# A three-layer macaron block on one core: attention's output sums leave by DMA on GpSimd's queue instead of through TensorE, and the next batches' LayerNorm and the queries' parts move to GpSimd

## What is computed

```python
x = x + 0.5 * ffn(layernorm(x))      # mixture of 8 experts, capacity 320, with a dense overflow path
x = x + attention(layernorm(x))
x = x + 0.5 * ffn(layernorm(x))
```

```python
xd = (x @ W_down).reshape(b, t, h, s)
keys = einsum('bthk,hik->bthi', xd, tokeys) * scale
queries = einsum('bthk,hik->bthi', xd, toqueries) * scale
values = einsum('bthk,hik->bthi', xd, tovalues)
attn = softmax(einsum('bqhs,bkhs->bhqk', queries, keys), axis=-1)
out = einsum('bhqk,bkhs->bqhs', attn, values).reshape(b, t, e)
return out @ W_unify + b_unify
```

## Time and profile before

| | |
|---|---|
| median of 3 runs | 2886.42 us |
| the profiled execution | 2896.95 us, its span 2895.2 us |
| attention, from the mask's first MEMSET to the last VectorE addition | 640.1 to 2259.1 us of the span |
| first exponential, last exponential | 707.1 and 2244.1 us |
| batches 1 to 6, first exponential to first exponential | 194.0 us each |
| batch 0 | 191.8 us |
| mean granted TensorE clock, whole program and inside batches | 0.964 and 1.00 |

### The profile page before, as it was taken

The page is one execution under the profiler, slowest core; times in us unless marked ns, Lnnn a source line. Parts: engine busy times, 40 slices in busy tenths (PEclk is TensorE's granted clock), DMA queues, the critical chain, the costliest instruction groups (busy, mean ns, idle before and its releaser), DMA issues. The chain is left out here.

```text
span 2895.2 us, 48611 instructions
## 1 busy us (share of the span) xinstructions
PE 2705.7 (93%) x17009; PEld 1644.3 (57%) x17009; DVE 2145.9 (74%) x3552; ACT 1821.3 (63%) x3409; POOL 599.8 (21%) x562
## 2 busy tenths in 40 slices
PE   5899999867999999999999999999999589999997
PEld 3799999863334334333343343433433368999886
DVE  6555456747899898998998988989895665554574
ACT  5344556632777776777777767777777444444564
POOL 3355114521100100101001001010000235521353
PEclk9899999986999999999999999999999789999998
DMA  5211113414123132131231321312310512111341
GB/s 172 66 44 44 58 45 106 133 60 75 30 50 75 33 61 54 39 62 36 50 75 33 60 55 39 62 37 50 60 28 5 173 30 80 44 44 45 102 133 63
DMA packets 164529, 181.69 MB, mean 63 GB/s; under 512 B 38472, under 2 KB 133904, under 8 KB 164368
## 3 DMA queue, kind: packets, MB, share of 16 engines
q1 hardware_dynamic: 156176, 169.03, 24.0%
q0 software_dynamic: 8192, 10.57, 1.2%
HBM read 97.51 MB, written 31.54 MB: 45 GB/s over the span
## 5 line engine op out<-in xcount | busy, mean ns | idle before, releaser
L1457 ACT ACTIVATE at_ex<-at_pd 128x512 f32<-128x512 f32 x2048 | 1084.7, 600 | 383.7 <-PE at_pd L1360 379.2
L1521 DVE TENSOR_REDUCE at_mxc<-at_pb 128x2 f32<-128x1024 f32 x1024 | 1219.0, 1219 | 120.8 <-PE at_pb L1349 113.8
L768 DVE TENSOR_TENSOR f_ml_hl<-f_ml_h,f_ml_hh 128x512 fp32r<-128x512 f32 (+1 forms) x384 | 287.8, 751 | 422.7 <-ACT f_ml_hh L844 421.5
L1360 PE MATMUL at_pd<-at_qa,at_ka 50*128 50x512 f32 x2048 | 583.6, 469 | 3.9 <-ACT at_ex L1457 3.2
L1360 PEld LDWEIGHTS at_pd<-at_qa,at_ka 50*128 50x128 f32 x2048 | 266.6, 185 | 538.4 <-issue 349.2
L1369 PE MATMUL at_po<-at_ex,at_va 128*32 128x512 f32 x4096 | 548.8, 608 | 0.2 <-ACT at_ex L1457 0.2
L841 ACT ACTIVATE f_ml_h<-f_ml_pL,b1T 128x512 f32<-128x512 f32 (+1 forms) x384 | 243.8, 635 | 457.9 <-PE f_ml_pL L895 446.3
L1349 PE MATMUL at_pb<-at_ka,at_qa 48*128 48x512 f32 x2048 | 433.1, 450 | 24.7 <-DVE at_mxc L1521 16.5
L910 PE MATMUL f_ml_pA<-f_wh,f_ml_hh 128*128 128x256 f32 (+1 forms) x1408 | 410.4, 291 | 3.7 <-DVE f_ml_hl L768 3.7
L912 PE MATMUL f_ml_pA<-f_wl,f_ml_hh 128*128 128x256 f32 (+1 forms) x1408 | 402.5, 286 | 0.0
L913 PE MATMUL f_ml_pA<-f_wh,f_ml_hl 128*128 128x256 f32 (+1 forms) x1408 | 402.5, 286 | 0.0
(11 more groups left out here) (128 smaller groups left out, 2636.6 us busy)
## 6 DMA issues: line engine op xcount, KB each, us to landing
f_wraw<-in_L_ffn_w SPq DMA_DIRECT2D x128, 256.0 KB, 2.8
at_qa<-at_parts SPq DMA_DIRECT2D x384, 64.0 KB, 2.4
at_ka<-at_parts SPq DMA_DIRECT2D x384, 64.0 KB, 2.4
f_ro_xr<-in_L_attn_x SPq DMA_DIRECT2D x16, 512.0 KB, 3.9
f_ml_xr<-in_L_attn_x SPq DMA_DIRECT2D x16, 512.0 KB, 4.2
x<-f_ml_yo SPq DMA_DIRECT2D x16, 512.0 KB, 4.0
at_xr<-x SPq DMA_DIRECT2D x16, 512.0 KB, 5.1
at_xres<-x SPq DMA_DIRECT2D x8, 1024.0 KB
```

Source lines behind the costliest of these rows:

```text
L768: eng.tensor_tensor(hl[h % RING][:, 0:w], h32[h % 2][:, 0:w], hh[h % RING][:, 0:w].bitcast(F32), ALU.subtract).then_inc(s_lo.sem, 1)
L1360: eng.matmul(pd[n % RING][:, :], ka[g][rows, p, kt * P:(kt + 1) * P], qa[g][rows, qh, p, :], start=True, stop=True).then_inc(s_full.sem, 1)
L1457: eng.activation(ex[t % 2][:, j, :], pd[n % RING][:, :], ACT.Exp).then_inc(s_free[n % RING].sem, 1)
L1521: eng.tensor_reduce(mxc[:, t // NT, kh, t % NT::NT], pb[kh][:, :].rearrange("p (e k) -> p e k", e=2), AX.X, ALU.max, negate=True).then_inc ...
```

## The change

- **The sums go by DMA.** `f` and `aT` leave the table. After `values_out` GpSimd issues, for each half unit, one DMA of `os_` to DRAM (`sums_out`), one that brings the totals back as 128 by 16 (`sums_in`, into `tot`), one that brings the values back already in the transposed place (`sums_in`, into `aT`). VectorE takes the reciprocal of `tot` (`reciprocals`, in step 4 or 12 of the half that follows), GpSimd stores it (`totals_out`) and reads it back spread over the 16 rows of each head (`totals_in`, into `den`). After two units' halves GpSimd multiplies `aT` by `den` (`divide`). The five DMAs and the multiplication stand in steps 0, 1, 5, 6 and 7 of the following half. Only the last half of the last batch goes the old way (`values_now`).
- **Output.** `u` of both halves is now in unit 0 of the next batch (steps 2, 3, 11, 12); of the last batch, half 0 is in steps 14 and 15 of unit 3.
- **LayerNorm a batch ahead.** Statistics of batch b + 2 are taken by VectorE in unit 0 (steps 13, 14) and unit 1 (steps 1, 2) of batch b, the variances in unit 2 (steps 2, 3); GpSimd normalises (`normalize`) in unit 2, steps 7 and 10.
- **Queries' parts.** ScalarE copies a `qk` bank to `xT` (freed by then), scaled; GpSimd makes both parts from there (`two_parts`).
- The bias is added to `xres` in unit 3 in two portions; `s_ld` and `s_mr` semaphores are merged; SyncE loads the rows of batch b + 3 in unit 3.

```diff
-        OUT = lambda f: [("aT", f, 0), ("aT", f, 1), ("u", f, 0), ("u", f, 1)]
+        PARTS = 2 * len(XD) + 2 * len(QK)
+        OUT = lambda f: [("u", f, 0), ("u", f, 1)]
...
-            table = {1: ("f", 1), 9: ("f", 0)}
-            if g == 0 and not prev:
-                del table[1]
+            table = {}
             if g == 0 and prev:
-                table.update(zip((2, 3, 5, 6), OUT(1)))
-            if g == 3:
-                table.update(zip((10, 11, 13, 14), OUT(0)))
+                table.update(zip((2, 3, 11, 12), OUT(0) + OUT(1)))
+            if g == 3 and last:
+                table.update(zip((14, 15), OUT(0)))
             if g == 0 and not last:
-                table.update(zip((7, 8, 10, 11, 13, 14), XT + XD))
+                table.update(zip((6, 7, 8, 9, 13, 14), XT + XD))
             if g == 1 and not last:
-                table.update(zip((2, 3, 5, 6, 7, 8), XD[-2:] + QK))
+                table.update(zip((1, 2, 5, 6, 7, 8), XD[-2:] + QK))
...
                 if j == 0:
-                    eng.wait_ge(s_free[n % RING].sem, s_free[n % RING].at(ring.freed(n)))
-                    eng.wait_ge(s_kp.sem, s_kp.at(2 * len(XD) * b + len(XD) * (c + 1)))
+                    eng.wait_ge(s_kp.sem, s_kp.at(PARTS * b + 2 * len(XD) + len(QK) * (c + 1)))
...
                 else:
                     f, h = a.at
+                    eng.wait_ge(s_dv.sem, s_dv.at(4 * a.b + 3 + f))
...
+            def reciprocals(b, g, qh):
+                eng.wait_ge(s_td.sem, s_td.at(16 * (half(b, g, qh) + 1)))
+                eng.reciprocal(tot[:, :], tot[:, :]).then_inc(s_rc.sem, 1)
...
             def values_out(b, g, t):
                 eng.wait_ge(s_pv.sem, s_pv.at(ST * unit(b, g) + t + 1))
+                if half(b, g, t // NT):
+                    eng.wait_ge(s_os.sem, s_os.at(16 * half(b, g, t // NT)))
                 eng.tensor_copy(os_[:, :], po[:, :]).then_inc(s_o.sem, 1)
...
-                    if g == 0 and not last and t < 8:
-                        f, q = t // 4, t % 4
-                        if q < 2:
-                            stats(b + 1, f, (FIRST, SECOND)[q])
-                        else:
-                            apply(self.ring, b + 1, f, side, (FIRST, SECOND)[q - 2])
+                    if t == NT + 4:
+                        reciprocals(b, g, 0)
+                    if t == 4 and (b or g):
+                        reciprocals(*before(b, g), 1)
+                    if (g, t) in STATS_AT and b + 2 < NBAT:
+                        stats(b + 2, STATS_AT[g, t])
+                    if (g, t) in VARIANCE_AT and b + 2 < NBAT:
+                        variance(b + 2, VARIANCE_AT[g, t])
...
+                eng.tensor_copy(parts[:, int(key), 0, c, at], src[:, c, at]).then_inc(s_kp.sem, 1)
+                eng.wait_ge(s_kp.sem, s_kp.at(n + 1))
+                eng.tensor_tensor(parts[:, int(key), 1, c, at], src[:, c, at], parts[:, int(key), 0, c, at].bitcast(F32),
+                                  ALU.subtract).then_inc(s_kp.sem, 1)
+
+            def normalize(ring, b, f, read):
+
                 if f == 0:
...
+                    norm.pow_step(eng, b, NT)
+                    eng.wait_ge(s_full.sem, s_full.at(ring.full(read)))
+                norm.apply_step(eng, b, xn, xr, [P] * NT, range(4 * f, 4 * f + 4)).then_inc(s_xn.sem, 1)
+
+            def sums_out(b, g, qh):
+                eng.wait_ge(s_o.sem, s_o.at(half(b, g, qh) + 1))
+                eng.dma_start(oscr[g, qh, :, :, :].rearrange("j r q -> (j r) q"), os_[:, :]).then_inc(s_os.sem, 16)
+
+            def sums_in(ring, b, g, qh, read):
+
+
+                eng.wait_ge(s_os.sem, s_os.at(16 * (half(b, g, qh) + 1)))
+                eng.dma_start(tot[:, :], oscr[g, qh, :, HS, :].rearrange("j (x y) -> j x y", y=HS)).then_inc(s_td.sem, 16)
+                if b > 0:
+                    eng.wait_ge(s_full.sem, s_full.at(ring.full(read)))
+                r0 = HS * GH * (g % 2)
+                eng.dma_start(aT[r0:r0 + HS * GH, qh, g // 2, :], oscr[g, qh, :, 0:HS, :]).then_inc(s_nd.sem, 16)
+
+            def totals_out(b, g, qh):
+                eng.wait_ge(s_rc.sem, s_rc.at(2 + half(b, g, qh) + 1))
+                eng.dma_start(rscr[g, qh, :, :].rearrange("j (x y) -> (j x) y", y=HS), tot[:, :]).then_inc(s_rs.sem, 16)
+
+            def totals_in(b, g, qh):
+
+                eng.wait_ge(s_rs.sem, s_rs.at(16 * (half(b, g, qh) + 1)))
...
+                eng.dma_start(den[r0:r0 + HS * GH, qh, :], src).then_inc(s_nd.sem, 16)
+
+            def divide(b, g, qh):
+
+                eng.wait_ge(s_nd.sem, s_nd.at(16 * 2 * (half(b, g, qh) + 1)))
+                if g % 2:
+                    eng.tensor_tensor(aT[:, qh, g // 2, :], aT[:, qh, g // 2, :], den[:, qh, :],
+                                      ALU.mult).then_inc(s_dv.sem, 1)
```

More of the change, by code:

```diff
@@ L148, in tile_stats, with aggregate @@
         return last
+    def aggregate(self, eng, n, rows, tiles):
+        for j, r in enumerate(rows):
+            if j in tiles:
+                last = eng.bn_aggr(self.mv[0:r, j, :], self.stats[0:r, j, :])
+        return last
     def stats_step(self, eng, n, src, rows, tiles=range(4)):
@@ L155, in stats_step, with variance @@
         eng.memset(self.pad[:, :], 0.0)
-        for j, r in enumerate(rows):
-            last = eng.bn_aggr(self.mv[0:r, j, :], self.stats[0:r, j, :])
-        last.then_inc(self.s_dve.sem, 1)
+        self.variance(eng, n, rows, range(len(rows)))
+    def variance(self, eng, n, rows, tiles):
+        self.aggregate(eng, n, rows, tiles).then_inc(self.s_dve.sem, 1)
         eng.wait_ge(self.s_dve.sem, self.s_dve.at(3 * n + 2))
@@ L1227, in phase, with units_landed @@
                     do.step(b, par, g, t, coming, tiles, done, a, side, ahead, last)
+        def units_landed(eng, b, c):
+            for g, p in ((0, 0), (0, 1), (1, 0)) if c == 0 else ((2, 0), (3, 0)):
+                eng.wait_ge(landed(g, p).sem, landed(g, p).at(loads(g, b)))
         block = ctx.enter_context(nc.Block())
@@ L1258, in load_head @@
                     eng.dma_start(ka[g][r1:r1 + HS, p, :].bitcast(F32),
[L1259 removed]
+                                  parts[r0:r0 + HS, 1, part, c, :].bitcast(F32)).then_inc(landed(g, p).sem, 16)
             def ones():
@@ L1682, in step @@
                 def step(self, b, par, g, t, coming, tiles, done, a, side, ahead, last):
-                    if g == 0 and not last and t in (1, 5):
-                        norm.pow_step(eng, 2 * (b + 1) + t // 4, 4)
-                    if a and a.kind == "xd":
-                        key_parts(self.ring, a)
-                    if g == 2 and t == 8:
+                    past = (b, g, 0) if t >= NT else (*before(b, g), 1) if b or g else None
+                    if past and t % NT == 0:
+                        sums_out(*past)
+                    if past and t % NT == 1:
+                        sums_in(self.ring, *past, self.read[past[2]])
+                    if past and t % NT == 5:
+                        totals_out(*past)
+                    if past and t % NT == 6:
+                        totals_in(*past)
+                    if g == 2 and t == 10 and b + 2 < NBAT:
+                        normalize(self.ring, b + 2, 1, side)
+                    if past and t % NT == 7:
+                        divide(*past)
+                    if g == 2 and t == 7 and b + 2 < NBAT:
+                        normalize(self.ring, b + 2, 0, side)
+                    if a and a.kind in ("xd", "qk"):
+                        two_parts(self.ring, a)
+                    if a and a.kind == "u":
+                        self.read[a.at[0]] = a.n
+                    if g == 3 and t in (2, 10):
                         eng.wait_ge(s_xl.sem, s_xl.at(16 * (8 + b + 1)))
-                        for q in range(0, NT, 2):
+                        for q in range(t // 8 * 4, t // 8 * 4 + 4, 2):
                             ins = eng.tensor_tensor(xres[:, q:q + 2, :], xres[:, q:q + 2, :],
```

257 lines of the change are left out of this document (129 added, 128 removed).

## The result

The changed kernel took 2872.53 us (median of 20 runs, 2861.49 to 2886.32) against 2888.89 us of the kernel before on the same chip: a ratio of 0.9945, interval 0.9929 to 0.9961. The direction was as forecast, the size was not: 16.4 us less between the medians, where 46.3 us had been expected. The profiled execution is the fastest of the 20, 2861.49 us.

What follows compares the result with a forecast made beforehand. The prediction took the attention step's loop through three banks as the bound. Terms -45.6 - 7.6 - 1.9 + 2.8 + 6.0 = -46.3 us gave 2840 us against the median 2886.42; range 2826 to 2872.

Steps and rivals of the forecast that it cites:

- The loop through the ring: Attention steps: matmul, exponential, fourth matmul waiting for its bank of three, times_v; 2.61 us a plain step, 3.10 with f.
- Rival (c): Attention steps: the bank is not what an f step costs; within 0.3% of before, 2886 us; chance 0.06 with other no-change causes.
- Terms 1 and 2: Walk: 93 f and aT steps become plain, 45.6 us less; VectorE's jam in unit 0 goes, 7.6 us less.
- Term 3: Tail behind the last step: one round of aT and the wait for its copy go, 1.9 us less.
- Term 4: Start: GpSimd makes two more pairs of parts before the first head load; 2.8 us more, ends 1.8 and 3.8.
- Term 5: Units 2 and 3: GpSimd's two-input operations hold VectorE's at_nm; 0.75 us a batch, 6 us more.
- The rule of the Trainium skill: VectorE with two SBUF inputs contends with any GpSimd SBUF read; some 16 operations more a batch, collision cost about 12 us.
- GpSimd's round: Sums, totals and division by DMA for each half unit: fits into the half, reciprocal 6 us to spare; costed at nothing.
- rival (b): GpSimd's round outlasts a half unit and VectorE's reciprocal waits; 2926 us at 5.5 us a landing; chance 0.11.
- The Trainium skill's 4 of 16 engines: Transfers of aT and den get 4 of 16 DMA engines; round estimated 0.9 us longer for den.
- Rival (a): VectorE becomes the bound, losing 0.5 us beyond its margin in every half unit; about 2872 us; chance 0.13.

Runs made afterwards that it cites:

- e6: e1 with a side product of one tiny matmul, taking a bank of the ring, in six plain steps of unit 2; 2874.86 us, one run.
- e7: e1 with four transposes, into PSUM the maxima use anyway, in each of six steps in a row; 2873.86 us, one run.
- e1: Changed kernel with GpSimd's bias additions three steps later in unit 3 (steps 5 and 13 for 2 and 10); 2842.08 us, ratio 0.9843.
- e9: e1 with a VectorE reduction of about 0.6 to 3.8 us, growing by batch, before at_nm in both halves of unit 3; 2892.38 us, one run.
- e0: The changed kernel run again, unedited; 2876.64 us, ratio 0.9952 against the kernel before.
- e5: e1 with four normalisings on GpSimd moved from unit 2 step 10 to unit 3 step 2, where at_nm is due; 2856.28 us, ratio 0.9857.
- e11: Changed kernel with the first bias addition of each half moved ahead of GpSimd's wait for the sums (steps 0 and 8); 2854.27 us, ratio 0.9886.
- e8: Changed kernel with bias additions placed singly at unit 3 steps 2, 4, 10, 12; in the trace still back to back; 2882.42 us, ratio 0.9943.
- e3: Changed kernel with the additions three steps later as in e1 and at_nm as a one-input reduction as in e2; 2844.89 us, ratio 0.984.
- e4: Changed kernel with all four bias additions of a batch in a row at unit 3 step 2; 2894.05 us, ratio 1.0005.
- e10: e1 with the parts of the queries' first two tiles of batch 0 made by VectorE instead of GpSimd; 2836.63 us, one run.
- e2: Changed kernel with at_nm as a reduction with one SBUF input, the additions where they were; 2871.49 us, ratio 0.9934.

## Why the prediction was right in direction and wrong in size

- **What bounds the kernel: right.** The loop through the ring is shown by e6 and e7. Rival (c) falls: with the bank alone a step gets its 0.49 us.
- **Terms 1 and 2, -45.6 and -7.6 us: right in the main, their total partly by luck.** In e1 the walk from first to last exponential step lasts 1481.6 us against 1534.2 before, 52.6 less, where the two terms give 53.2. No L1378-type transposes are left in the walk. But by the prediction's own prices 50.6 of the 53.2 us lie in batches 0 to 6 (81 `f` and `aT` steps, term 2, and two `u` steps that move on into batch 7), and there it is 45.1. Batches 1 to 5 last 187.9 us in e1, and only batch 6 comes near the forecast 187.2, with 187.3. The difference is step 5 of unit 1: 3.46 us in the batches that have statistics in that unit, 2.79 in batch 6, which has none, 2.61 before. There a held `at_nm` and a pair of statistics follow each other on VectorE; the prediction had both at no cost. The last batch gives most of that back, 7.4 us in place of 2.6, and in no term's way: in the one profiled execution of the kernel before, the granted clock is at half for 10.2 us of the last unit, whose steps 8 to 10 take 3.80, 4.07 and 4.11 us in place of 2.61, 2.61 and 3.10. In e1 it is at half nowhere in that unit. The unit before, 45.9 us with a mean clock of 0.89:

```profile
2195.39:2241.29 45.90, 42.73 (x221) 14.89 (x219) 13.30 (x19) 32.29 (x62) 0.00 (x0) 0.89 0.01 3
```

- **Term 3, -1.9:** 17.8 us from the last step to the end of the attention became 17.1, so -0.7; in e1 it is 15.6. The executions scatter by more than the term.
- **Term 4, +2.8: undersized.** 67.0 us from the start of the attention to the first exponential became 70.8: +3.8, the upper end, and 71.3 in e1. The two pairs ahead of the first head load are there as forecast, 26.8 us from the start to this load became 30.6 (it stands at 666.48 and not near 670, since this execution reached the attention 4.2 us earlier). The 1 us for shared statistics didn't come back: GpSimd's first pair begins 19.1 us after the start, before it was 19.2.
- **Term 5, +6 us: the step that failed.** "One hit of 0.79 us in every half unit" was my worst case for one hold and "VectorE's margin of 1.1 us in a half unit hides most of one hit" my reason to stay low. Both were wrong in size. A hold isn't one operation of GpSimd but all that stand in a row, 2.5 us of additions and up to 0.8 us before them: 3.3 us. The margin at that place is 0.42 us (e9); that it is one step's and not the mean of eight is my reading of this. And behind one of the two stalls of 1.74 us and behind every longer one TensorE's clock falls, which no term had. In place of 6 us, unit 3 lost 23.5 us against 41.7 a batch in the changed kernel's profiled execution, the fastest of its 20 runs, and 31.0 in e0's; between the medians of e0 and e1 it is 34.6.
- **The sum without term 5 is -52.3 us.** e1 measures -45.4 (0.0157 of 2890.73; -39 to -52 by its interval), and -48.7 between the medians. That this is close to the recorded -46.3 confirms nothing, since term 5 is in that. The parts that fell short are the 5.5 us in batches 0 to 6 and the 1.0 to 1.5 us of term 4.
- I had read the earlier trace rows as the size of the effect. It was the size of one operation with nothing behind it: GpSimd's next starts 2.3 us after its end. The kernel before had all four bias additions in a row too (in batch 3 from 1390.79 to 1395.77 us), but between one `at_nm` at 1378.99 and the next at 1400.37.
- The rule of the Trainium skill, weighed in term 5 at 12 us, didn't rescue it: it counts more operations, and e5 shows that the normalisings slow VectorE a little and don't hold it. What was missing was the length of a row of them.
- **Costed at nothing, GpSimd's round: right, with wrong parts.** Issues take 0.59 to 0.70 us (1.0 assumed), landings 2.1 to 4.3 (3), normalising 1.21 us (0.3 to 0.6), the power 1.67 (1.0). Its slack of 6.8 us took the difference; rival (b) didn't come.
- The Trainium skill's 4 of 16 engines ("DMA: Bandwidth & Descriptors", "Why a DMA increments its semaphore by 16 and not by 1") fits: `aT` and `den`, 128 KB each, land in 4.0 and 4.3 us, `oscr` with 256 KB in 2.4. The 0.9 us more that the prediction had estimated from it is less than this difference. No run changed the shapes of these transfers, so the cause is argued, not shown.
- **Rival (a)**, 2872 us by collisions, gave the measured number and the right engine, but as a steady loss in every half unit; it is a few large ones in unit 3. I gave it 0.13. What the profile allowed me to ask was: which small operation of VectorE stands in the path of the maxima, and which operations of GpSimd can be in a row beside it?

## What to carry to other kernels

When work moves to GpSimd, list its two-input operations that stand back to back, and the small SBUF operations of VectorE that a chain waits for. Their collision costs the whole row, not one operation, and a stall that lets TensorE run dry is paid again at 1.2 GHz. Keep rows short, put them where a wait fixes their time away from the chain, and read where they fall in the trace: the number of a step says nothing on an engine that waits elsewhere.

## What the runs showed that I had not expected

A hold of VectorE can begin before GpSimd's addition by the record: 0.77 us in the changed kernel, 0.7 in e11, both times inside a DMA issue ahead of it, though issues with no addition behind them leave `at_nm` at 0.18 us. In e8 an `at_nm` that starts 0.97 us ahead of an addition takes 0.18 us too. Whether the lock is taken so early, or GpSimd's starts are recorded late, stays open.

The clock of the last unit, where `for_max` is over, decides over 14 us. The same 197 matmuls, in e5 and in e1:

```profile
2149.20:2202.70 53.50, 50.13 (x197) 14.02 (x195) 11.73 (x17) 31.20 (x61) 13.57 (x16) 0.63 0.08 22
```

```profile
2150.30:2189.40 39.10, 34.04 (x197) 10.73 (x196) 11.75 (x16) 31.06 (x61) 13.37 (x16) 1.00 0.11 31
```

In e5 and e7 it took 53.5 and 53.7 us, in the changed kernel, e1, e3, e4, e10 and e11 39.1 or less, and 44.7 to 50.6 in e0, e2, e6, e8 and e9. At full clock, TensorE is busy for 34.04 of 39.1 us there, where plain steps with `for_max` fill it. Since e0 and the changed kernel are one program, it needs no edit to change; a part of the 14 us between e1 and e5 may be just that. What sets it off was not tried.

The FFNs, which no edit touched, scatter as well: in the 14 profiled executions the program takes 635.7 to 641.3 us up to the attention and 631.5 to 636.1 us behind it. The one execution of the kernel before has 640.1 and 636.1, near the upper ends, so a profile of it against another overstates a gain by a few microseconds.
